# Tail of the single head's scores as two bfloat16 matmuls over three-part splits

## The chip, the cores and the metric

The kernel runs on one core of one Trainium2 chip. The metric is device time in microseconds (us) of one execution. Five engines run their own instruction streams and meet at semaphores: PE (TensorE, matrix multiplies; PEld is its loading of weights), DVE (VectorE), ACT (ScalarE), POOL (GpSimd, here the engine that issues the row gathers) and SP (SyncE, here the engine that issues all other transfers; SPq is its queue). Transfers run on 16 DMA engines.

## The reference

A graph of 12,500 nodes and 200,000 edges, the edges sorted by destination. Three message-passing steps follow one another: an attention pooling, a transformer convolution with 8 heads, and one with a single head of width 128.

```python
h = relu(layernorm(x));  x = x + pooled(h)            # step 1: softmax over edges of logit[src]
h = relu(layernorm(x));  x = x + conv1(relu(conv8(h)))
# a convolution, per edge s -> d with edge features e (16 numbers):
q, k, v = h @ Wq + bq, h @ Wk + bk, h @ Wv + bv
alpha = sum(q[d] * (k[s] + e @ We)) / sqrt(C)          # the score
w = softmax over the edges of d (alpha)
out[d] = sum(w * (v[s] + e @ We)) + h[d] @ Ws + bs
```

For the single head the kernel folds the key weights into the query: the score of an edge is the product of a column of 145 numbers of node `d` (128 against `h[s]`, 16 against `e`, one against a constant 1) and the row of the edge. The 128 are the main part, the 17 (`TAIL`) the tail.

## The kernel before

**Stages.** The program is written out in full, stage after stage, with a barrier between them: `prepare`, `hidden_stage`, `dense_stage("pool")`, `project_stage`, `edge_stage("multi")`, `fold_stage`, `dense_stage("single")`, `output_stage`.

**Dense stages.** Edges are cut into 391 blocks of 512 (`J` = 4 groups of 128), nodes into 98 tiles of 128. An item is a pair of a block and a tile that share edges; there are 488, in the order of the edges. Since low-numbered nodes have most of the edges, an item is nearly a block of its own at first, and a block has more and more items towards the end. POOL gathers the source rows, four gathers a block (L1155), into a ring of 8 blocks, as far ahead as the ring has room (it waits for `rows`, the copy by ACT at L1300 of the last item of the block that it overwrites). Everything else goes by item and is software-pipelined over up to three items: in `"single"` PE turns the rows (`ps_r`, L1265), makes the scores from `cols` (128x128) and `rowT` (L1251) plus `cols_tail` and `edge_tail` (L1253, 17 rows deep, float32), turns the weights (`ps_t`, L1278) and sums (`ps_p`, L1271); DVE does mask, minimum, copy and accumulation; ACT the exponentials and copies. In `"pool"` the scores are only a transpose (L1258).

**Transfers.** SP issues five transfers an item in `"single"`, in this order: `dst` (L1178), `cols` (L1183), `cols_tail` (L1185), `edge_tail` (L1189, 17 rows of 2 KB), the edge attributes (L1191). It runs at most four items (`QB`) ahead of the scores, since `cols` waits for the score of item n - 4; `dst` and the edge buffers are 8 deep (`U`).

**Fold.** `fold_stage` goes over 14 batches of 7 node tiles (`ROWS_B`). For a batch, SP loads `skip` and `x` (L1557, L1558), DVE makes `h` (L1585 to L1603), PE turns it (L1625), and multiplies; ACT copies `hT` (L1651), and then, for the batch before, `query_main` and `query_tail` (L1657, L1658). SP stores `h`, `x`, `query_main` and `query_tail` of the batch before (L1562 to L1568). SP loads a batch only when all four stores of two batches earlier have landed (L1556): a store and a load of one buffer share a semaphore's count.

Of the kernel before, what the change touches and what calls it, by code (L numbers as in the profile page):

```python
# [22 lines left out]
BF16 = mybir.dt.bfloat16  # L23
# [3 lines left out]
ds = bass.ds  # L27
# [32 lines left out]
DEN_EPS = 1e-16  # L60
assert ITEMS % U == 0 and NODE_TILES % ROWS_B == 0 and BATCHES % 2 == 0

# [89 lines left out]
def buffers(g):  # L152
# [14 lines left out]
    g.query_cols = scratch("query_cols", [SLOTS, ACC_W, P])  # L167
# [237 lines left out]
def hidden_stage(g):  # L405
# [8 lines left out]
    with ExitStack() as ph:  # L414
# [22 lines left out]
        def _(sp):  # L437
# [10 lines left out]
            sp.dma_start(g.query_cols[NODE_TILES, D:ACC_W, :], zero_cols[0:TAIL, :]).then_inc(s_w, 16)  # L448
# [5 lines left out]
            sp.wait_ge(s_w, 80)  # L454
# [211 lines left out]
def edge_stage(g, kind, rows, width, heads, ring_blocks):  # L666
# [404 lines left out]
    for k in EDGE_SIGNALS:  # L1071
        used = {"kv": multi, "attrT": multi, "edge": multi, "attrT_sb": multi, "scaled": multi,
                "prod": not pool_k, "alpha": not pool_k, "query": not pool_k, "onehot32": multi, "rows": not multi}.get(k, True)
        E[k].base += ITEMS if used else 0
# [15 lines left out]
def dense_stage(g, kind, rows, width, ring_blocks):  # L1090
# [16 lines left out]
    with ExitStack() as ph:  # L1107
# [10 lines left out]
        if single:  # L1118
            rowT = sb(g, ph, "rowT", [P, 2, EDGES_B])
            cols = sb(g, ph, "cols", [P, QB, P])  # L1120
            cols_tail = sb(g, ph, "cols_tail", [TAIL, QB, P])
            edge_tail = sb(g, ph, "edge_tail", [TAIL, U, EDGES_B])
            ps_r = [pb(g, ph, f"ps_r{k}", [P, EDGES_B]) for k in range(2)]
        ps_s = [pb(g, ph, f"ps_s_{kind}{k}", [P, EDGES_B]) for k in range(2)]
# [45 lines left out]

        @block.sync
        def _(sp):
            items = Items(g, sp, 0)

            def step(n, u):
                b = items.block(u)
                E["mask"].wait(sp, n - U)
                sp.dma_start(dst[:, u], t["dst_rows"][ds(b, 1), :].to_broadcast([P, EDGES_B]))\  # L1178
                  .then_inc(g.block_words_loaded[u], 16)
                if single:  # L1180
# [4 lines left out]
                    sp.dma_start(cols_tail[:, u % QB],  # L1185
                                 g.query_cols[ds(tile, 1), D:ACC_W, :].rearrange("t c n -> (t c) n"))\
# [7 lines left out]
            rolled(sp, ITEMS, U, 0, step, items.begin)  # L1194

        @block.vector
        def _(dve):
            items = Items(g, dve, 2)
            if single:
                V.memset(row[:, :, :, ACC_W - 1:ACC_W], 1.0)  # L1200
            V.memset(g.acc[:], 0.0)
# [3 lines left out]
            def step(n, u):  # L1205
# [26 lines left out]
                if has(m1, ITEMS):  # L1232
# [3 lines left out]
                     .then_inc(E["probT_sb"].sem, 1)  # L1236
            rolled(dve, ITEMS, U, 2, step, items.begin)

        @block.tensor
        def _(pe):  # L1240

            def step(n, u):
# [3 lines left out]
                if has(m1, ITEMS):  # L1246
                    E["low"].wait(pe, m1 - 2)
                    if single:
                        E["rowT_sb"].wait(pe, m1)
                        landed(pe, g.query_loaded, query_base, m1, u1, 32)  # L1250
# [544 lines left out]
```

## Time and profile before

| | |
|---|---|
| three runs | 10781.99, 10849.4 and 10866.37 us, median 10849.4 |
| span of the profiled execution (first to last instruction) | 7414.1 us |
| PE busy in the span | 5718.3 us (77%) |
| DVE, ACT, POOL busy | 4663.7 (63%), 3438.6 (46%), 4576.5 us (62%) |
| moved by DMA | 861.45 MB, mean 116 GB/s |

The span holds the instructions of the program. The difference to the run time, 3435.3 us, lies around it, and no view of the profile shows anything of it. The profiled execution's own device time is not listed apart. Busy shares are averages over stages that differ, so the stages have to be read one by one. Times below are counted from the span's start.

### The profile page before, as it was taken

Reading aid. Unit: us, or ns where it says so; the run is one execution under the profiler, and the core shown is the slowest. Engines: PE = TensorE matmul, PEld = TensorE weight load, DVE = VectorE, ACT = ScalarE, POOL = GpSimd, SP = SyncE. Lnnn points to the kernel's source line nnn. Section 1 sums busy time; section 2 is a strip of 40 time slices with the busy share of each in tenths; the row PEclk is TensorE's granted clock in tenths of the full one; section 3 lists DMA queues with packets and bytes.
Section 4 is the critical chain, followed back from the end, with each engine's and each line's share of the span. In section 5 each row is a group of like instructions: output and inputs, shape, how many; then the busy total and the mean of one; then the engine's idle time right before and its main releaser. Section 6 shows DMA issues by size and latency. Waiting matters only on the chain. (4 is left out here: it accounts for less than half of the span.)

```text
span 7414.1 us, 172328 instructions
## 1 busy us (share of the span) xinstructions
PE 5718.3 (77%) x38285; PEld 4085.0 (55%) x38285; DVE 4663.7 (63%) x12926; ACT 3438.6 (46%) x8180; POOL 4576.5 (62%) x4707
## 2 busy tenths in 40 slices
PE   4555566666665688888888888856889999999998
PEld 3455555555542466666666666633555556666666
DVE  4444555555665788999999999933444555555542
ACT  3233333333443466666666666612444444444441
POOL 0777777777750477777666665502777777777630
PEclk7777878888986799999999999977999999999995
DMA  2334444444434666666655555534445555555532
GB/s 81 85 82 83 85 85 87 88 89 89 92 90 140 161 155 157 159 158 153 151 144 145 142 140 137 130 103 119 108 110 112 117 116 119 123 122 123 119 88 60
DMA packets 1267854, 861.45 MB, mean 116 GB/s; under 512 B 637234, under 2 KB 1158320, under 8 KB 1266840
## 3 DMA queue, kind: packets, MB, share of 16 engines
q1 hardware_dynamic: 1091672, 438.53, 25.3%
q0 software_dynamic: 175168, 411.90, 23.7%
q8 instruction: 332, 5.44, 0.3%
q14 instruction: 682, 5.59, 0.3%
HBM read 780.46 MB, written 69.42 MB: 115 GB/s over the span
## 5 line engine op out<-in xcount | busy, mean ns | idle before, releaser
L757 POOL DMA_INDIRECT ring_multi<-kv_rows,src_cols x1564 | 1609.3, 1029 | 1029.7 <-issue 440.4
L1155 POOL DMA_INDIRECT ring_single<-h_rows,src_cols x1564 | 1482.6, 948 | 857.2 <-issue 480.3
L1155 POOL DMA_INDIRECT ring_pool<-pool_rows,src_cols x1564 | 1482.0, 948 | 678.6 <-issue 451.5
L1258 PE MATMUL ps_s_pool<-ident,row_pool 128*128 128x128 f32 x1952 | 365.1, 319 | 718.0 <-ACT row_pool L1300 716.8
L1300 ACT ACTIVATE row_pool<-ring_pool 128x520 f32 x488 | 309.1, 633 | 1162.1 <-POOLq L1146 1162.1
L958 PE MATMUL ps_e_multi<-w_edge,attrT 64*128 64x512 f32 x976 | 544.5, 638 | 331.4 <-DVE kv L847 310.9
L1222 DVE CUSTOM_DVE_ANT_0 masked_pool<-mask_pool,ps_s_pool,start_pool 128x512 f32<-128x512 bf16 x488 | 364.8, 748 | 633.4 <-PE ps_s_pool L1258 552.3
L1271 PE MATMUL ps_p_pool<-row_pool,probT_pool 128*128 128x129 f32 x3904 | 667.1, 325 | 55.2 <-DVE probT_pool L1235 54.2
L847 DVE TENSOR_TENSOR kv<-ring_multi,ps_e_multi 128x1024 f32<-128x1024 f32 x488 | 596.1, 1222 | 161.6 <-issue 124.0
L1258 PEld LDWEIGHTS ps_s_pool<-ident,row_pool 128*128 128x128 f32 x1952 | 254.1, 160 | 801.5 <-issue 764.9
L1305 ACT ACTIVATE rowT<-ps_r 128x512 f32<-128x512 f32 x488 | 291.7, 598 | 816.4 <-PE ps_r L1265 816.4
L1271 PEld LDWEIGHTS ps_p_pool<-row_pool,probT_pool 128*128 128x128 f32 x3904 | 602.7, 235 | 97.5 <-DVE probT_pool L1235 97.2
L1222 DVE CUSTOM_DVE_ANT_0 masked_single<-mask_single,ps_s_single,start_single 128x512 f32<-128x512 bf16 x488 | 364.7, 747 | 427.8 <-PE ps_s_single L1253 424.3
L948 PE MATMUL ps_p_multi<-message_multi,onehot 128*128 128x136 f32 x3904 | 584.2, 297 | 0.5 <-issue 0.4
L1271 PE MATMUL ps_p_single<-row_single,probT_single 128*128 128x145 f32 x3904 | 581.1, 292 | 2.4 <-DVE probT_single L1235 2.4
L1253 PE MATMUL ps_s_single<-edge_tail,cols_tail 17*128 17x512 f32 x976 | 549.7, 643 | 0.0
L948 PEld LDWEIGHTS ps_p_multi<-message_multi,onehot 128*128 128x128 f32 x3904 | 536.7, 207 | 0.9 <-issue 0.7
L1271 PEld LDWEIGHTS ps_p_single<-row_single,probT_single 128*128 128x128 f32 x3904 | 525.2, 194 | 3.6 <-DVE probT_single L1235 2.8
L1251 PE MATMUL ps_s_single<-rowT,cols 128*128 128x512 f32 x976 | 512.2, 607 | 1.5 <-issue 1.5
L1230 DVE SCALAR_TENSOR_TENSOR acc<-acc,factor_single,ps_p_single 128x145 f32 x488 | 178.9, 367 | 521.0 <-PE ps_p_single L1271 513.4
L1265 PEld LDWEIGHTS ps_r<-ident,row_single 128*128 128x128 f32 x1952 | 207.9, 142 | 493.1 <-issue 255.7
L1300 ACT ACTIVATE row_single<-ring_single 128x512 f32 x488 | 304.2, 623 | 294.5 <-POOLq L1146 292.0
(218 smaller groups left out, 12218.1 us busy)
## 6 DMA issues: line engine op xcount, KB each, us to landing
dst_pool<-in_dst_rows SPq DMA_DIRECT2D x488, 128.0 KB
dst_multi<-in_dst_rows SPq DMA_DIRECT2D x488, 128.0 KB
dst_single<-in_dst_rows SPq DMA_DIRECT2D x488, 128.0 KB
query_multi<-query_parts SPq DMA_DIRECT2D x488, 96.0 KB
cols<-query_cols SPq DMA_DIRECT2D x488, 64.0 KB
ring_pool<-pool_rows,src_cols POOLq DMA_INDIRECT x1564
ring_multi<-kv_rows,src_cols POOLq DMA_INDIRECT x1564
ring_single<-h_rows,src_cols POOLq DMA_INDIRECT x1564
```

Source lines behind the costliest of these rows:

```text
L757: pool.indirect_dma_start(out=ring[:, u, j, :], out_offset=None, in_=rows, in_offset=bass.IndirectOffsetOnAxis(ap=g.src_cols[:, c:c + 1], ...
L847: V.tensor_tensor(out=kv[:, u1 % 4], in0=in_ring(items.block(m1), 0, 2 * D).rearrange("p j (a c) -> p j a c", a=2), in1=ps_e[:].rearrange( ...
L948: i = T_.matmul(ps_p[:, 0:acc_w], lhs, rhs, start=(j == 0), stop=(j == J - 1))
L958: T_.matmul(ps_e[:], attrT[:, u % 2], w_edge[:].rearrange("k j c -> k (j c)"), start=True, stop=True).then_inc(E["edge"].sem, 1)
L1155: pool.indirect_dma_start(out=ring[:, u, j, :], out_offset=None, in_=rows, in_offset=bass.IndirectOffsetOnAxis(ap=g.src_cols[:, c:c + 1], ...
L1222: V.tensor_tensor_reduce(out=masked[:, p], in0=mask[:, p], in1=ps_s[p][:], scale=1.0, scalar=start[:, p], op0=ALU.add, op1=ALU.min, accum_ ...
L1251: T_.matmul(ps_s[p1][:], cols[:, u1 % QB], rowT[:, p1], start=True, stop=False)
L1253: T_.matmul(ps_s[p1][:], cols_tail[:, u1 % QB], edge_tail[:, u1], start=False, stop=True)\
L1258: i = T_.transpose(ps_s[p1][:, j * P:(j + 1) * P], row[:, u1, j, D + 1:D + 2].to_broadcast([P, P]), g.ident[:])
L1271: i = T_.matmul(ps_p[p3][:, 0:acc_w], probT[:, p3, j], row[:, u3, j, 0:acc_w], start=(j == 0), stop=(j == J - 1))
L1300: S_.activation(row[:, u, :, 0:copied], in_ring(items, u, 0, copied), ACT.Copy)\
L1305: S_.activation(rowT[:, u % 2], ps_r[u % 2][:], ACT.Copy).then_inc(E["rowT_sb"].sem, 1)
```

## The change

The tail's factors are each written as a sum of three bfloat16 numbers (`SPLIT` = 3: the number rounded, the rest rounded, the rest of that). All nine products are summed by two matmuls in bfloat16: `tail_a` (99 rows: the first and the second part of the query, each against the edge's three parts, and three rows against ones) and `tail_b` (48 rows: the third part of the query against the edge's three parts).

- **Single:** the float32 matmul of L1253 is replaced by two bfloat16 ones. SP issues six transfers an item in place of five: `cols`, `tail_a` (99 rows of 256 bytes), `tail_b` (48 rows of 256 bytes), and `edge_tail` as 96 rows of 1 KB, which reads the same 48 rows of `edge_parts` twice by a source pattern whose outer dimension is 2 with step 0. PE waits for DVE's clearing of buffers before its first item.
- **Pool:** between the items, every 12th, one of 40 chunks (128 x 626 numbers) of the edge attributes is loaded (SP, 12.8 MB in all), split in two ACT copies and two DVE subtractions, and stored (SP, 19.2 MB in all).
- **Fold:** after `query_tail`, DVE makes its three parts in five operations on 17 x 896 numbers, and SP stores them in 12 transfers a batch in place of one; loads wait for three stores in place of four.
- **Inputs:** `edge_cols` (17 x 200,192 float32, 13.61 MB) gives way to `edge_flat` (128 x 25,040 float32, 12.82 MB).

```diff
@@ dense_stage, single
-            cols_tail = sb(g, ph, "cols_tail", [TAIL, QB, P])
-            edge_tail = sb(g, ph, "edge_tail", [TAIL, U, EDGES_B])
+            tail_a = sb(g, ph, "tail_a", [TAIL_A, QB, P], BF16)
+            tail_b = sb(g, ph, "tail_b", [SPLIT_K, QB, P], BF16)
+            edge_tail = sb(g, ph, "edge_tail", [TAIL_A, U, EDGES_B], BF16)
...
+                i = chunk(n, 0)
+                if i is not None:
+                    if i >= 2:
+                        sp.wait_ge(third_done, i - 1)
+                    sp.dma_start(whole[:, i % 2], t["edge_flat"][:, i * CHUNK_W:(i + 1) * CHUNK_W])\
+                      .then_inc(split_loaded[i % 2], 16)
+                i = chunk(n, 18)
+                if i is not None:
+                    sp.wait_ge(third_done, i + 1)
+                    sp.dma_start(split_rows[:, :, i * CHUNK_W:(i + 1) * CHUNK_W], split[:, i % 2])\
+                      .then_inc(split_stored[i % 2], 16)
...
-                    sp.dma_start(edge_tail[:, u], t["edge_cols"][:, ds(b * EDGES_B, EDGES_B)])\
-                      .then_inc(g.attrs_loaded[u], 16)
+                    sp.dma_start(edge_tail[0:2 * SPLIT_K, u], g.edge_parts[:, ds(b * EDGES_B, EDGES_B)]
+                                 .unsqueeze(0).to_broadcast([2, SPLIT_K, EDGES_B])).then_inc(g.attrs_loaded[u], 16)
...
-                        T_.matmul(ps_s[p1][:], cols_tail[:, u1 % QB], edge_tail[:, u1], start=False, stop=True)\
+                        T_.matmul(ps_s[p1][:], tail_a[:, u1 % QB], edge_tail[:, u1], start=False, stop=False)
+                        T_.matmul(ps_s[p1][:], tail_b[:, u1 % QB], edge_tail[0:SPLIT_K, u1], start=False, stop=True)\
                           .then_inc(E["score"].sem, 1)
@@ fold_stage, SP
                     sp.dma_start(tiles[0:D], main[:, v]).then_inc(stored[v], 16)
-                    sp.dma_start(tiles[D:ACC_W], tail[:, v]).then_inc(stored[v], 16)
+                    sp.wait_ge(tail_part, 5 * (k + 1))
+                    rows = g.query_tails[k * ROWS_B:(k + 1) * ROWS_B].rearrange("t c n -> c t n")
+                    for a in range(SPLIT):
+                        for r in range(SPLIT):
+                            at = (a * SPLIT + r) * EDGE_DIM + (SPLIT if a == SPLIT - 1 else 0)
+                            sp.dma_start(rows[at:at + EDGE_DIM], tails[0:EDGE_DIM, v, a]).then_inc(tails_stored[v], 16)
+                        at = 2 * SPLIT_K + a
+                        sp.dma_start(rows[at:at + 1], tails[EDGE_DIM:TAIL, v, a]).then_inc(tails_stored[v], 16)
@@ fold_stage, DVE
+                    D_["query_done"].wait(dve, k)
+                    V.tensor_copy(tails[:, v, 0], tail[:, v]).then_inc(tail_part, 1)
+                    for a in range(SPLIT - 1):
+                        V.tensor_tensor(out=tail[:, v], in0=tail[:, v], in1=tails[:, v, a], op=ALU.subtract)\
+                         .then_inc(tail_part, 1)
+                        V.tensor_copy(tails[:, v, a + 1], tail[:, v]).then_inc(tail_part, 1)
```

PE, where the single stage has come into step (an item's rows, its scores, the sums of three items earlier, the weights of two earlier). Before:

```order
L1265 MATMUL ps_r<-ident,row_single 128x128 x4
L1278 MATMUL ps_t_single<-ident,prob_single 128x128 x4
L1251 MATMUL ps_s_single<-rowT,cols 128x512
L1253 MATMUL ps_s_single<-edge_tail,cols_tail 128x512
L1265 MATMUL ps_r<-ident,row_single 128x128 x4
```

After:

```order
L1323 MATMUL ps_r<-ident,row_single 128x128 x4
L1336 MATMUL ps_t_single<-ident,prob_single 128x128 x4
L1308 MATMUL ps_s_single<-rowT,cols 128x512
L1310 MATMUL ps_s_single<-edge_tail,tail_a 128x512
L1311 MATMUL ps_s_single<-edge_tail,tail_b 128x512
L1323 MATMUL ps_r<-ident,row_single 128x128 x4
```

Nothing moved; one row of the tail became two. SP, one batch of `fold_stage` (names are tensors in memory and buffers; `query_tails_sb` are the three parts), before:

```order
L1557 DMA skip<-skip_rows 128x7x128
L1558 DMA x<-x_rows 128x7x128
L1562 DMA h_rows<-h 128x7x128
L1564 DMA skip_rows<-x 128x7x128
L1567 DMA query_cols<-query_main 128x7x128
L1568 DMA query_cols<-query_tail 17x7x128
```

After:

```order
L1628 DMA skip<-skip_rows 128x7x128
L1629 DMA x<-x_rows 128x7x128
L1633 DMA h_rows<-h 128x7x128
L1635 DMA skip_rows<-x 128x7x128
L1638 DMA query_cols<-query_main 128x7x128
L1644 DMA query_tails<-query_tails_sb 16x7x128 x3
L1646 DMA query_tails<-query_tails_sb 7x1x128
L1644 DMA query_tails<-query_tails_sb 16x7x128 x3
L1646 DMA query_tails<-query_tails_sb 7x1x128
L1644 DMA query_tails<-query_tails_sb 16x7x128 x3
L1646 DMA query_tails<-query_tails_sb 7x1x128
L1628 DMA skip<-skip_rows 128x7x128
```

Twelve rows now stand between the store of `query_main` and the next batch's loads, where one stood. DVE in the same batch, the end of a batch, after the change:

```order
L1682 TENSOR_TENSOR x<-x,bs 128x896
L1689 TENSOR_TENSOR x<-x,ps_z 128x896
L1694 CAST query_tails_sb<-query_tail 17x896
L1697 TENSOR_TENSOR query_tail<-query_tail,query_tails_sb 17x896
L1700 CAST query_tails_sb<-query_tail 17x896
L1697 TENSOR_TENSOR query_tail<-query_tail,query_tails_sb 17x896
L1700 CAST query_tails_sb<-query_tail 17x896
L1664 TENSOR_SCALAR den<-acc 128x56
```

Before, `den` followed the addition of `ps_z` to `x` (L1689, which was L1610) directly; the five rows between are new.

## Rows read from the trace of the kernel before

**Rows 1.** Busy time by stage: stretch, length, each engine's busy (instructions), clock, DMA, GB/s
```profile
178.00:2178.00 2000.00, 1221.86 (x7837) 1095.43 (x7836) 1082.62 (x2959) 711.58 (x1467) 1482.03 (x1564) 0.84 0.41 86
...
5120.00:7200.00 2080.00, 1968.11 (x9760) 1209.04 (x9760) 1077.23 (x2931) 959.65 (x1952) 1482.64 (x1564) 0.98 0.53 115
```

**Rows 2.** The same view, stretches inside the single stage
```profile
5130.00:5700.00 570.00, 496.51 (x2343) 304.07 (x2343) 261.39 (x707) 238.95 (x474) 422.65 (x447) 0.94 0.50 110
5700.00:6300.00 600.00, 573.82 (x2844) 352.45 (x2842) 311.32 (x855) 281.25 (x568) 443.43 (x468) 0.98 0.54 117
6300.00:6900.00 600.00, 600.00 (x3058) 368.97 (x3058) 333.31 (x916) 295.53 (x612) 445.75 (x471) 1.00 0.56 123
6900.00:7142.00 242.00, 242.00 (x1230) 148.16 (x1229) 133.89 (x370) 117.93 (x245) 163.21 (x173) 1.00 0.54 118
```

**Rows 3.** Waits of POOL, single stage, then pool stage: total, times, longest
```profile
POOL ring_single L1155 <- issue: 480.3, 1468, 3.0
POOL ring_single L1155 <- ACT row_single L1300: 34.7, 30, 2.3
...
POOL ring_pool L1155 <- issue: 450.0, 1435, 2.0
```

**Rows 4.** Timeline: ends of the pool stage and of the single stage, start and length
```profile
2162.89 0.95 POOL L1155 DMA_INDIRECT ring_pool<-pool_rows,src_cols  x1 [0.30 <-issue]
2177.01 0.35 DVE L1230 SCALAR_TENSOR_TENSOR acc<-acc,factor_pool,ps_p_pool 128x129 f32 x1 [1.53 <-PE ps_p_pool L1271]
...
7141.74 0.95 POOL L1155 DMA_INDIRECT ring_single<-h_rows,src_cols  x1 [0.30 <-issue]
7198.21 1.26 PE L1271 MATMUL ps_p_single<-row_single,probT_single 128*128 128x145 f32 x8 [1.59 <-DVE probT_single L1235]
```

**Rows 5.** Timeline of PE: one item, and bfloat16 matmuls of the multi stage
```profile
6502.69 1.02 PE L1251 MATMUL ps_s_single<-rowT,cols 128*128 128x512 f32 x2
6503.64 1.12 PE L1253 MATMUL ps_s_single<-edge_tail,cols_tail 17*128 17x512 f32 x2
6504.70 0.66 PE L1265 MATMUL ps_r<-ident,row_single 128*128 128x128 f32 x4
6506.62 1.02 PE L1251 MATMUL ps_s_single<-rowT,cols 128*128 128x512 f32 x2
...
4755.39 0.83 PE L994 MATMUL ps_q_multi<-query_multi,onehotT_multi 128*128 128x128 bf16 x12
```

**Rows 6.** SP from 6300 to 6900: its wait, and from its timeline two issues
```profile
SPq L1183 <- PE ps_s_single L1253: 139.6, 149, 1.2
...
6501.70 0.25 SPq L1185 DMA_DIRECT2D cols_tail<-query_cols  x1
6502.15 0.25 SPq L1189 DMA_DIRECT2D edge_tail<-in_edge_cols  x1
```

**Rows 7.** DMA queues from 6300 to 6900: packets, MB, share of 16 engines
```profile
q1 hardware_dynamic: 129826, 41.72, 32.3%
```

**Rows 8.** Timeline of a batch of the fold stage: stores, then the next loads
```profile
4986.56 0.38 SPq L1567 DMA_DIRECT2D query_cols<-query_main  x1
4986.99 0.41 SPq L1568 DMA_DIRECT2D query_cols<-query_tail  x1
4992.63 0.37 SPq L1557 DMA_DIRECT2D skip<-skip_rows  x1
4993.65 0.56 SPq L1562 DMA_DIRECT2D h_rows<-h  x1
4997.96 0.25 DVE L1585 TENSOR_SCALAR den<-acc 128x56 f32<-128x56 f32 x1 [13.79 <-DMA x<-x_rows]
```

**Rows 9.** Fold stage: SP's wait for stores, and two groups of DVE by line
```profile
SPq L1556 <- DMA query_cols<-query_tail: 61.5, 12, 5.2
...
L1592 DVE TENSOR_TENSOR h<-acc,den 128x896 f32<-128x896 f32 x14 | 15.3, 1093 | 1.8
L1601 DVE TENSOR_SCALAR h<-h 128x896 f32<-128x896 f32 x14 | 8.8, 627 | 0.5
```

More of the change, by code:

```diff
@@ L60 @@
 DEN_EPS = 1e-16
+SPLIT = 3
+SPLIT_K = SPLIT * EDGE_DIM
+CHANNEL = EDGES + P
+FLAT = EDGE_DIM * CHANNEL // P
+CHUNK_W = 626
+SPLITS = FLAT // CHUNK_W
+EVERY = 12
+TAIL_A = 2 * SPLIT_K + SPLIT
+TAIL_ROWS = TAIL_A + SPLIT_K
 assert ITEMS % U == 0 and NODE_TILES % ROWS_B == 0 and BATCHES % 2 == 0
+assert SPLITS * CHUNK_W == FLAT and (SPLITS - 1) * EVERY + 18 < ITEMS
 def rolled(eng, total, unroll, lag, step, begin=None, peel=None):
@@ L1169, in landed, with chunk @@
             eng.wait_ge(sems[u % len(sems)], n * per + (per_item - (u % len(sems)) * per + base))
+        def chunk(n, at):
+            i, r = divmod(n - at, EVERY)
+            return i if not single and r == 0 and 0 <= i < SPLITS else None
         @block.sync
@@ L1194, in _ @@
             rolled(sp, ITEMS, U, 0, step, items.begin)
+            if not single:
+                for k in range(2):
+                    sp.wait_ge(split_stored[k], 16 * len(range(k, SPLITS, 2)))
         @block.vector
@@ L1236, in step @@
                      .then_inc(E["probT_sb"].sem, 1)
+                i = chunk(n, 5)
+                if i is not None:
+                    dve.wait_ge(first_done, i + 1)
+                    V.tensor_tensor(out=whole[:, i % 2], in0=whole[:, i % 2], in1=split[:, i % 2, 0], op=ALU.subtract)\
+                     .then_inc(first_off, 1)
+                i = chunk(n, 9)
+                if i is not None:
+                    dve.wait_ge(second_done, i + 1)
+                    V.tensor_tensor(out=split[:, i % 2, 2], in0=whole[:, i % 2], in1=split[:, i % 2, 1],
+                                    op=ALU.subtract).then_inc(third_done, 1)
             rolled(dve, ITEMS, U, 2, step, items.begin)
@@ L1240, in _ @@
         def _(pe):
+            if single:
+                pe.wait_ge(g.acc_clear, 3)
             def step(n, u):
@@ L1305, in step @@
                         S_.activation(rowT[:, u % 2], ps_r[u % 2][:], ACT.Copy).then_inc(E["rowT_sb"].sem, 1)
+                i = chunk(n, 3)
+                if i is not None:
+                    act.wait_ge(split_loaded[i % 2], 16 * (i // 2 + 1))
+                    if i >= 2:
+                        act.wait_ge(split_stored[i % 2], 16 * (i // 2))
+                    S_.activation(split[:, i % 2, 0], whole[:, i % 2], ACT.Copy).then_inc(first_done, 1)
+                i = chunk(n, 7)
+                if i is not None:
+                    act.wait_ge(first_off, i + 1)
+                    S_.activation(split[:, i % 2, 1], whole[:, i % 2], ACT.Copy).then_inc(second_done, 1)
             rolled(act, ITEMS, U, 2, step, items.begin)
@@ L1312, in dense_stage @@
     g.attrs_base += ITEMS * 32 // U if single else 0
-    g.query_base += ITEMS * 32 // QB if single else 0
+    g.query_base += ITEMS * 48 // QB if single else 0
 def waits_of_buffer(eng, sems, base, n, u):
@@ L1526, in fold_stage @@
         tail = sb(g, ph, "query_tail", [TAIL, 2, ROWS_B, P])
+        tails = sb(g, ph, "query_tails_sb", [TAIL, 2, SPLIT, ROWS_B, P], BF16)
+        tail_part = sem(g, "tail_part")
+        tails_stored = [sem(g, f"tails_stored{k}") for k in range(2)]
         wq = sb(g, ph, "wq2", [P, D])
```

49 lines of the change are left out of this document (35 added, 14 removed).

## Prediction

> **What bounds the kernel now.** I read the busy time by stage first [rows 1]. The single stage takes 2080 us of the 7414.1 us span, PE is busy in 1968 of them, and the change takes work from PE: that looks like a large gain. The pool stage corrects the picture: POOL issues the same 1564 gathers there, is busy for the same 1482 us, and that stage lasts 2000 us with PE busy in only 1222. A gather costs POOL 0.95 us and some 0.3 us up to the next [rows 4], so about 1.27 us, or 5.1 us a block. That alone is 1990 us of the single stage.
>
> Then the single stage in stretches [rows 2]. An item has 20 matmul records on PE (4 for `ps_r`, 2 and 2 for the scores, 4 for `ps_t`, 8 for `ps_p`), so the four stretches hold 117, 142, 153 and 61.5 items: 4.87, 4.22, 3.92 and 3.93 us an item. The gathers go at 78.4, 78.0, 78.5 and only in the last stretch at 71.5 per 100 us. So gathers set the pace up to 6300 us; from there PE is busy all the time and falls behind, the ring of 8 blocks takes up the lag, and only near the end does POOL wait for a freed block: 34.7 us in 30 waits [rows 3]. The rest of the lag is the drain: from the end of the last gather (7142.7 us) to the last item 57 us in the single stage, in the pool stage 13 us (2163.8 to 2177) [rows 4].
>
> So the most that a faster item can bring: some 8 gathers lie ahead of 5130 us (the stage starts at 5120) and 447 + 468 up to 6300; 641 are left. At 600/471 = 1.274 us each [rows 2] they end at 7117, with the pool stage's drain 7130, against 7199.5 now: **70 us**. In items: 488 - 117 - 142 = 229 are left after 6300 us and take 900 us now, 3.93 each. With p us an item the stage ends 900 - 229 p earlier, up to 70 us (p = 3.62 or less). Before 6300, p up to 4.2 costs nothing.
>
> **The change, part by part.** *Scores.* The tail's float32 matmul holds PE from 6503.64 to 6504.70, 1.05 us [rows 5]; it is four passes of 512 columns in two records. Two bfloat16 matmuls are two passes. Twelve bfloat16 ones of 128 columns take 0.83 us, 69 ns each with their weights [rows 5]; by columns that is at most 0.28 us for 512, so 0.55 for two; the least is half of the tail's time less its overheads, 0.45. I take 0.5, which saves 0.55: PE alone would need 3.4 us an item. The Trainium skill, "TensorE: Matmul & The Clock Gate", section "Back-to-back issue gap", gives N / 2.4 + 2.5 ns warm; by it the two take 0.43 us and PE would need 3.3 us. No row here has a bfloat16 matmul of 512 columns.
>
> *SP in the single stage.* From 6300 to 6900 us SP waits 139.6 us over 153 items, 0.91 us each [rows 6], so it works 3.0 us an item. One transfer more costs the spacing of `cols_tail` and `edge_tail`, 0.45 us [rows 6], and the two larger ones some 0.05 each: 3.55 us. SP passes from 23% to almost no slack, and becomes the next limit at the end, just where it is enough (3.62).
>
> *The copy of the edges.* 34 KB an item become 96 KB. I leave a margin for it and for waits that come when nothing has slack: p = 3.75, a gain of 900 - 859 = **41 us**. Bounds: 70, and nothing at p = 3.93.
>
> *More traffic.* The chunks add 32 MB to the pool stage, the tails and edges 91 KB an item (44 MB) to the single stage, 16 and 21 GB/s on 86 and 115 [rows 1]. The gaps that go to issue are 450.0 us in the pool stage at a DMA share of 0.41 and 480.3 in the single stage at 0.53 [rows 1, 3]. 30 us for 0.12; the new traffic is about 0.05 in each: up to 12 us. I take **+6** twice; bounds 0 and 12. The chunks' two ACT copies and two DVE subtractions each 12 items lie beside POOL's gathers, which leave PE, ACT and DVE 39% and more idle there [rows 1]; without that cover they would cost some 40 x 3 us.
>
> *Fold.* Here nothing hides anything. Per batch SP stores `query_main` at 4986.56 and `query_tail` at 4986.99, waits for the landing, and loads the next but one at 4992.63: 6.07 us [rows 8]; the wait is 61.5 us in 12 batches [rows 9]. DVE then idles until 4997.96 for that load. The wait goes, since loads ask for three stores only and that of `query_main` lands meanwhile. In its place, in order on SP: 0.42 for `query_main`; DVE's five operations, which start when `query_tail` is there, 3 casts and 2 subtractions of 896 numbers, a subtraction 1.09, a cast between 0.63 and 1.09 [rows 9], so 4.1 to 5.5, and 0.3 for the hand-overs; then 12 issues, nine at 0.41 (as `query_tail`'s) and three at 0.25 [rows 6, 8], each 0.05 apart: 5.0. Together 9.8 to 11.2 against 6.07. I take +4.2 for 12 batches, 50 us, and 9 for the last, whose tail now follows the DVE work: **+59 us**. Bounds: 12 issues at 0.25 and cheap casts, +2.2 a batch and 33 us in all; 12 at 0.56 [rows 8] and dear casts, +7.4 and 101 us. Queued behind SP's new wait are the next loads, for which all engines wait. DVE, waiting for `query_tail`, has nothing else due before that load.
>
> **Sum.** -41 + 59 + 6 + 6 = +30 us on the span of 7414.1. The profiled execution's 3435.3 us outside the span are taken as unchanged, and the median of the runs stands for its time: 10849.4 + 30, about **10,880 us**.
>
> **Rivals.**
> (a) *Slower: the copy of `edge_tail` becomes the bound.* If its rows don't spread over the 16 DMA engines, one engine carries much of 96 rows. For it: the source pattern has an outer dimension of 2. With two engines, 48 rows of 1 KB each. A packet of q1 takes 32.3% x 16 x 600 us / 129,826 = 23.9 ns at a mean of 321 bytes [rows 7]; 1 KB costs between that and 76 ns (by bytes), so 1.15 to 3.7 us. An engine has now 0.56 x 3.92 = 2.2 us an item [rows 2]. Sum 3.3 to 5.9 us; at 4.4 the stage ends 229 x 4.4 - 900 = 108 later, and 142 x (4.4 - 4.22) = 25 more: +133 in place of -41, in all +204, **11,053 us**; at 5.9 about 800. It makes the kernel over 1% slower from p = 4.1 on. Against it: transfers 8 deep hide any latency, and the lower half of the price is below what PE takes now. The Trainium skill, "DMA: Bandwidth & Descriptors", section "Why a DMA increments its semaphore by 16 and not by 1", says that the engine count is the largest number up to 16 that divides the slowest dimension of both patterns, which would be 2 here (and 1 for the present copies of 17 rows). No row shows the count.
> (b) *The gain is whole and fold cheap.* Spread copy, p under 3.62, fold at its lower bound: -70 + 33 = **10,812 us**. Against it: SP at 3.55.
> (c) *The time around the span shrinks.* The inputs lose 0.79 MB of some 42 MB in and out. If the 3435 us went by bytes, that is 65 us: **10,815 us**. Nothing in the profile speaks for or against it.
> (d) *PE's clock.* It is 0.98 to 1.00 in the last stretches and 0.94 where PE is busy for 87% of the time [rows 2]. If the shorter item lets it fall to 0.94 at the end, 3.4 becomes 3.6 us: within the forecast.
>
> **How the numbers follow.** Forecast 0.62 (all within 1%), (a) 0.2, (b) 0.1, (c) 0.08. Over 1% (108 us) is about what can be told from no change. Slower by that: (a), and a fold at its upper bound together with no gain, 0.21. Faster: (b) and (c) together, 0.04. Within: 0.75. The range reaches down a little beyond (b) and (c) and up to the middle of (a): 10,790 to 11,030; the forecast's own is 10,810 to 10,950.
>
> **What would show it.** In the single stage: two records of 0.25 us for the tail; an item at 3.6 to 3.9 us after 6300; gathers at 78 per 100 us to the end, POOL's waits for ACT's rows under 10 us; a drain of 20 to 40 us. SP's wait for the scores gone there. If instead PE waits for a DMA of `edge_tail`, (a) holds. In the fold stage: each batch 3 to 5 us longer, SP's wait names DVE and not the stores. In the pool stage: the same length within 15 us. The prediction is wrong if PE was the real pace before 6300 (the stage would then shrink by far more than 70 us), or if a chunk's store holds up gathers.

## The result, and the profile after

| | median of 20 runs | range |
|---|---|---|
| kernel before | 10850.4 us | 10777.6 to 10905.6 |
| changed kernel | 10877.4 us | 10817.3 to 10934.5 |

The ratio is 1.0036, 95% interval 1.0019 to 1.0053: taken on 10,850 us, 39 us more, between 21 and 58 (the two medians by themselves differ by 27). The change is below 1% and the time is inside the range of the prediction; its +30 is inside the interval.

The profile after shows at once that much of the prediction's ground does not hold for these runs. The changed kernel's profiled execution takes 10889.8 us and its span is 10888.0 us. So next to nothing (1.8 us) lies around the span; the 3435.3 us that the section on the time before put around the span, and that the prediction left "outside", are inside, in the stages with gathers. The execution that the rows of before were read from was an untypical one: a second profile of the unchanged kernel (`b0` below) has a span of 10601.3 us in 10603.2.

Busy time by stage, pool, multi and single (the columns as in [rows 1]). The changed kernel:

```profile
190.00:3107.00 2917.00, 1349.82 (x7800) 1213.56 (x7800) 1123.05 (x3009) 753.28 (x1544) 1490.03 (x1564) 0.71 0.30 69
3405.00:7105.00 3700.00, 2625.23 (x19030) 1952.44 (x19031) 2233.82 (x5861) 1542.46 (x4393) 1529.97 (x1564) 0.72 0.37 94
7448.00:10674.00 3226.00, 2157.79 (x9758) 1381.34 (x9759) 1070.82 (x2930) 955.50 (x1952) 1480.52 (x1564) 0.81 0.39 88
```

The same view of `b0`, the unchanged kernel:

```profile
192.00:3055.00 2863.00, 1355.77 (x7807) 1219.45 (x7808) 1070.03 (x2929) 699.82 (x1464) 1477.53 (x1564) 0.71 0.27 60
3352.00:6936.00 3584.00, 2600.01 (x19031) 1938.11 (x19032) 2232.29 (x5858) 1538.93 (x4393) 1521.99 (x1564) 0.73 0.39 97
7215.00:10388.00 3173.00, 2481.77 (x9759) 1480.57 (x9760) 1073.73 (x2929) 948.08 (x1952) 1478.05 (x1564) 0.81 0.33 75
```

In `b0` the busy times of DVE, ACT and POOL are within 2% of those of [rows 1]; PE's is 11% larger in the pool stage and 26% in the single stage, at a lower clock. The pool stage is 2863 us long in place of 2000, the single stage 3173 in place of 2080. POOL is busy for 52% and 47% of them, not for 74% and 71%. (The two profiles are from different chips. On the one of the result the kernel before takes 10,850 us, on the one of `b0` 10,573, so stages are compared only within a chip.)

Waits in the single stage, the changed kernel, then `b0` (total, times, longest):

```profile
ACT rowT L1363 <- remote: 1415.8, 171, 20.3
POOL ring_single L1178 <- ACT row_single L1358: 1225.4, 214, 12.4
...
PE ps_s_single L1310 <- DMA row_single<-in_edge_attr: 37.5, 32, 2.9
...
SPq L1230 <- PE ps_p_single L1329: 14.1, 31, 0.7
SPq L1230 <- remote: 0.5, 3, 0.2
SPq L1217 <- DVE mask_single L1257: 0.3, 1, 0.3
```

```profile
POOL ring_single L1155 <- ACT row_single L1300: 1132.2, 190, 11.1
ACT rowT L1305 <- remote: 1105.2, 140, 30.3
...
SPq L1183 <- PE ps_s_single L1253: 514.3, 272, 4.1
SPq L1183 <- remote: 336.2, 114, 5.0
```

Three things are to be seen. POOL waits over 1100 us for a free block (34.7 in [rows 3]), so in these runs its gathers don't set the pace. ACT waits over 1100 us for `ps_r` with nothing in the profile that is still at work, which the view calls remote. And SP, which waits 852 us in the single stage of `b0`, waits 15 us in all after the change.

What "remote" is, in the timeline of the changed kernel (start, length, [idle before]):

```profile
9000.08 0.60 PE L1336 MATMUL ps_t_single<-ident,prob_single 128*128 128x128 f32 x4
9001.38 0.38 PE L1310 MATMUL ps_s_single<-edge_tail,tail_a 99*128 99x512 bf16 x1
9001.69 0.39 PE L1311 MATMUL ps_s_single<-edge_tail,tail_b 48*128 48x512 bf16 x1
9002.01 0.66 PE L1323 MATMUL ps_r<-ident,row_single 128*128 128x128 f32 x4
9007.18 0.69 DVE L1280 COPY probT_single<-ps_t_single 128x512 f32<-128x512 f32 x1 [5.58 <-remote]
9009.44 0.60 ACT L1363 ACTIVATE rowT<-ps_r 128x512 f32<-128x512 f32 x1 [8.25 <-remote]
```

The transposes into `ps_t` are recorded as done at 9000.68, those into `ps_r` at 9002.67. The semaphores with which PE tells so rise at 9007.15 and 9009.42, and DVE and ACT start 0.03 us later. From 9002.67 to 9007.15 no compute engine works. Counting each rise of a semaphore that comes over 1 us after the end of the record it belongs to:

| | pool | multi | single |
|---|---|---|---|
| PE, execution of [rows 1 to 9] | 0 | 0 | 0 |
| PE, `b0` | 548 | 1245 | 689 |
| PE, changed kernel | 528 | 1146 | 747 |
| DVE, all three | 0 | 0 | 0 |

The end of a matmul's record is modelled, so the trace can't tell whether PE's signal is late or the matmul itself stands still. The Trainium skill, "Perfetto Trace Analysis", section "Tensor Engine Instruction (MATMUL, LD_WEIGHTS)", says the same of the recorded end: an estimate from size and delay, not an observation. Below, "late" means late against the record. The traces also lack some of the rises (12% to 21% of PE's in the ordinary executions, 3% in that of [rows 1 to 9], about 30% of DVE's in `b0` and the changed kernel), so the counts are lower bounds.

### The profile page after: what moved, and what is told of

The parts are those of the page before. It is cut to its first block and busy times, and to the rows that moved or that the text cites. A ratio compares the mean times of both kernels' runs of the same rounds, so it can differ in the third digit from the quotient of the medians.

```text
span 10888.0 us, 173824 instructions
## 1 busy us (share of the span) xinstructions
PE 6690.3 (61%) x38285; PEld 4886.5 (45%) x38285; DVE 4855.3 (45%) x13077; ACT 3475.6 (32%) x8260; POOL 4503.1 (41%) x4707
## 5 line engine op out<-in xcount | busy, mean ns | idle before, releaser
L971 PE MATMUL ps_e_multi<-w_edge,attrT 64*128 64x512 f32 x976 | 754.1, 863 | 859.4 <-ACT attrT L1051 551.2
L1349 ACT ACTIVATE prob_pool<-masked_pool,low_pool 128x512 f32<-128x512 f32 x488 | 352.2, 722 | 2016.3 <-DVE low_pool L1267 1722.2
L1329 PE MATMUL ps_p_single<-row_single,probT_single 128*128 128x145 f32 x3904 | 710.8, 334 | 388.4 <-DVE probT_single L1280 310.5
L961 PE MATMUL ps_p_multi<-message_multi,onehot 128*128 128x136 f32 x3904 | 760.0, 357 | 0.5 <-issue 0.4
L961 PEld LDWEIGHTS ps_p_multi<-message_multi,onehot 128*128 128x128 f32 x3904 | 719.7, 267 | 0.8 <-issue 0.6
L971 PEld LDWEIGHTS ps_e_multi<-w_edge,attrT 64*128 64x128 f32 x976 | 187.0, 238 | 1004.7 <-ACT attrT L1051 799.1
L1275 DVE SCALAR_TENSOR_TENSOR acc<-acc,factor_pool,ps_p_pool 128x129 f32 x488 | 170.1, 348 | 1038.2 <-remote 795.9
L1007 PE MATMUL ps_q_multi<-query_multi,onehotT_multi 128*128 128x128 bf16 x5856 | 572.2, 270 | 0.0
L1280 DVE COPY probT_single<-ps_t_single 128x512 f32<-128x512 f32 x488 | 336.1, 689 | 500.5 <-remote 431.0
L1063 ACT ACTIVATE absent_multi<-ps_m_multi,neg_big 128x4 f32<-128x4 f32 x488 | 128.7, 264 | 1203.4 <-PE ps_m_multi L998 705.3
```

The source lines that it names most:

```text
L961: i = T_.matmul(ps_p[:, 0:acc_w], lhs, rhs, start=(j == 0), stop=(j == J - 1))
L971: T_.matmul(ps_e[:], attrT[:, u % 2], w_edge[:].rearrange("k j c -> k (j c)"), start=True, stop=True).then_inc(E["edge"].sem, 1)
L1007: i = T_.matmul(ps_q[:, j], onehotT[:, u, j], query[:, u % QB, k, 0:D], start=(k == 0), stop=(k == 2))
L1275: V.scalar_tensor_tensor(out=a2, in0=a2, scalar=factor[:, f2], in1=ps_p[p2][:, 0:acc_w], op0=ALU.mult, op1=ALU.add).then_inc(E["summed"].s ...
L1280: V.tensor_copy(probT[:, p1].rearrange("p j n -> p (j n)"), ps_t[p1][:])\
L1329: i = T_.matmul(ps_p[p3][:, 0:acc_w], probT[:, p3, j], row[:, u3, j, 0:acc_w], start=(j == 0), stop=(j == J - 1))
```

## The experiments

Stage lengths below run from the first gather (or the end of the stage ahead) to the last `ps_p` matmul or the next first gather. The first four kernels ran on one chip (before: 10,572.6 us), the next four on one where before took 10,567.8 us, the last four on one with 10,818.6 us. A stage's length is from the one profiled execution of a kernel, the ratio from all its runs. The unchanged kernel was profiled on the first chip only; on the second, `notail` has before's pool and multi stages, and they take 2861 and 3576 us there against `b0`'s 2863 and 3585, so `b0`'s stages are used for the second chip too.

**What each part of the change costs.** `b0` is the kernel before:

> The kernel before, unchanged. Two theories on the time that the profile of before did not show. (O) outside: the 3435 us lie around the instructions; then this execution's span is again near 7414 us while its time is near 10,850 us. (W) waits: the profiled execution of before was an untypical one, and ordinary ones have the 3435 us inside, as stalls in which PE, DVE, ACT and SP all do nothing for 2 to 9 us, as the changed kernel's profile shows them (span 10,888.0 us of a time of 10,889.8 us); then span and time differ by some 2 us, the pool stage takes near 2,900 us and not 1,985, and the single stage near 3,200 us.

Theory W holds: the span is 10,601.3 us of 10,603.2, the pool stage takes 2863 us and the single stage 3174.

`nofold` leaves the twelve stores and the five DVE operations out and fills the tails with zeros ahead; `nochunk` the chunks; `neither` both.

```diff
@@ nofold, fold_stage
-                    V.tensor_copy(tails[:, v, 0], tail[:, v]).then_inc(tail_part, 1)
...
-                            sp.dma_start(rows[at:at + EDGE_DIM], tails[0:EDGE_DIM, v, a]).then_inc(tails_stored[v], 16)
@@ nochunk, dense_stage
-            return i if not single and r == 0 and 0 <= i < SPLITS else None
+            return None
```

> The changed kernel without the chunks of the pool stage (the edge parts are an input of zeros) and without the three parts of the query's tail (they stay zero, written once in the hidden stage): the scores' tail is left out of the computation, the single stage does all its transfers and matmuls. It shows the change in the single stage by itself. Prediction's theory (gathers set the pace, PE's gain 41 us, traffic +6): 35 us faster than before, ratio 0.997. Rival 1 (stalls set the pace and shrink with the work on PE's path): 0.5 us less an item on 488 items, 240 us faster, ratio 0.978. Rival 2 (one more transfer an item on SP, whose register instructions take 0.7 us in places, costs what PE gains): ratio 1.000 to 1.01.

> The changed kernel without the three parts of the query's tail in the fold stage (no five DVE operations and no 12 stores a batch; the tails stay zero). Prediction's theory: the fold stage returns to its time of before and this is 59 us faster than the changed kernel (ratio to before 0.998). Rival (the fold stage has the same time as its loads wait in either): equal to the changed kernel, ratio 1.0036.

> The changed kernel without the 40 chunks of the pool stage (the edge parts are an input of zeros). Prediction's theory: hidden behind the gathers, 6 us, ratio 1.003. Rival (the pool stage isn't bound by the gathers but by waits among PE, ACT and DVE, and each chunk puts some 3 us on them): 40 to 120 us faster than the changed kernel, ratio 0.993 to 1.000.

| us | ratio to before, 95% | hidden | pool | multi | fold | single |
|---|---|---|---|---|---|---|
| `b0` | 1 | 192 | 2863 | 3585 | 278.4 | 3174 |
| `neither` | 1.0029 (1.0010 to 1.0049) | 234 | 2876 | 3619 | 239.3 | 3200 |
| `nofold` | 1.0022 (1.0004 to 1.0040) | 232 | 2853 | 3562 | 243.7 | 3168 |
| `nochunk` | 1.0075 (1.0052 to 1.0097) | 194 | 2879 | 3595 | 342.5 | 3204 |

- The fold stage costs +64.1 us. Without splits and stores it is 35 to 39 us shorter than before, so these alone cost 99 to 103. The removed wait for `query_tail` by itself is worth about 20 of the 35 to 39: `paced_best` below, which drops only that wait, has 258. `nofold` and `neither` also lack the one store of the tail; the rest was not taken apart.
- The single stage, the same program in all three, is 5 us shorter to 30 us longer than before. The multi stage, which is before's own, differs by -23 to +34 between executions, so that is within noise. The runs say the same: the ratios less what the fold and hidden stages account for leave +28, +18 and +13 us for all the rest, each within some 20 to 25. A gain of 41 us from the two bfloat16 matmuls does not show on this chip.
- The chunks cost nothing that these runs show (pool 2853 with, 2876 and 2879 without; by the runs, `nofold` with them and `neither` without have ratios of 1.0022 and 1.0029). `nochunk` itself, at 1.0075, is outside what either theory expected, and above the changed kernel's 1.0036, which was measured on another chip. The +40 in the hidden stage is the filling with zeros, which only `nofold` and `neither` have.

**Is PE's work on the path?** `notail` is the kernel before without the float32 matmul of the tail.

```diff
-                        T_.matmul(ps_s[p1][:], cols[:, u1 % QB], rowT[:, p1], start=True, stop=False)
+                        T_.matmul(ps_s[p1][:], cols[:, u1 % QB], rowT[:, p1], start=True, stop=True)
-                        T_.matmul(ps_s[p1][:], cols_tail[:, u1 % QB], edge_tail[:, u1], start=False, stop=True)\
```

> The kernel before without the tail's float32 matmul (the 17 rows of the tail are left out of the scores; all transfers, waits and copies stand). It takes 1.05 us an item from PE, twice what the change takes, 488 x 1.05 = 512 us in all. Theory A (the single stage's items wait for late signals and not for PE's work): under 100 us shorter. Rival D (PE's work is on the path of every item): 400 to 510 us shorter, about 10,100 us, and the change should then have gained about 250.

The stage in `notail`, then in `nochunk`, the changed program's:

```profile
7205.00:10245.00 3040.00, 1837.08 (x8784) 1348.45 (x8784) 1069.30 (x2929) 958.38 (x1952) 1481.88 (x1564) 0.78 0.34 79
7303.00:10507.00 3204.00, 2161.49 (x9752) 1388.55 (x9752) 1073.42 (x2930) 954.77 (x1952) 1478.52 (x1564) 0.80 0.40 89
```

Ratio 0.9878 (0.9843 to 0.9913), single stage 3041 us in place of 3174. PE's busy time falls by 645 us and the stage by 133, a fifth. That is between what both theories expected: neither "nothing" nor "all" holds. For the change, which takes 320 us of busy time off PE (2161.5 in `nochunk` against 2481.8), a fifth would be 66 us. Whether something takes them back or they are lost among the late signals, these kernels don't tell.

**What makes the late signals?** They occur only in stages with gathers, and in `b0`'s pool stage the share of time with no compute engine at work is at most 0.01 where POOL was busy with gathers for less than 30% of the last 5 us, 0.39 where it was for 60 to 70% and 0.61 for 70 to 80%. So three kernels put a pause between gathers: `pace_short` and `pace_long` on the kernel before (384 and 896 numbers), `pace_after` on the changed one (384).

```diff
                     ).then_inc(gathered[n % 2][j], 16)
+                    if g.pauses >= 2:
+                        pool.wait_ge(g.paused, g.pauses - 1)
+                    pool.memset(pause[:, g.pauses % 2], 0.0).then_inc(g.paused, 1)
+                    g.pauses += 1
```

> The kernel before with a pause on POOL: after every gather of the pool, multi and single stages POOL clears a scratch row of 384 numbers (one partition; by the row of the clearing of 488 numbers, 0.50 us, and of 128, 0.19 us, about 0.4 us). Gathers then start at least some 1.6 us apart in place of 1.25. Nothing else is changed. Theory A (gathers that follow each other without a pause hold up what the other engines tell each other): the idle stretches of 2 to 9 us in which no compute engine works become few; pool stage 2550 to 2700 us (it was 2863), single stage 2600 to 2900 (3174), multi 3000 to 3400 (3585), in all 9,400 to 10,300 us. Rival B (each gather costs the others the same wherever it stands): the same number of gathers, the same idle time: 10,500 to 10,700 us. Rival C (POOL is the pace and its waits for a free block are no slack): 1564 x 0.35 us more in each of three stages, 12,000 us and over.

> As the short pause, with a cleared row of 896 numbers, about 0.9 us: gathers at least 2.1 us apart. Theory A: the idle stretches are gone nearly wholly, but POOL alone now needs 1564 x 2.1 = 3300 us a stage, so about 10,900 us in all, with PE's longest waits in the dense stages for POOL's blocks. Rival B: the idle stretches stay and add to that, 11,500 us and over.

> The changed kernel with the short pause. Theory A: it gains what the kernel before gains from the same pause, and what the change does is seen with few stalls: fold stage again 60 to 65 us longer than before; the single stage, where PE is a larger part of the time, 0 to 100 us shorter than that of the kernel before with the pause. Rival B: as the changed kernel, 10,600 to 10,700 us on this chip.

POOL's timeline, `b0`, then `pace_short`:

```profile
1499.16 0.94 POOL L1155 DMA_INDIRECT ring_pool<-pool_rows,src_cols  x1 [0.30 <-issue]
1500.41 0.94 POOL L1155 DMA_INDIRECT ring_pool<-pool_rows,src_cols  x1 [0.30 <-issue]
```

```profile
1500.35 0.95 POOL L1163 DMA_INDIRECT ring_pool<-pool_rows,src_cols  x1 [0.16 <-issue]
1501.29 0.41 POOL L1169 MEMSET pause_pool<- 1x384 f32 x1
1501.86 0.95 POOL L1163 DMA_INDIRECT ring_pool<-pool_rows,src_cols  x1 [0.16 <-issue]
```

| | us | ratio to before, 95% | period of gathers | pool | multi | single | late in pool, multi, single |
|---|---|---|---|---|---|---|---|
| `b0` (first chip) | 10603, one run | 1 | 1.25 | 2863 | 3585 | 3174 | 548, 1245, 689 |
| `pace_short` | 9386 | 0.8853 (0.8813 to 0.8894) | 1.52 | 2412 | 3469 | 2526 | 6, 1083, 730 |
| `pace_long` | 10336 | 0.9766 (0.9724 to 0.9808) | 1.95 | 3061 | 3227 | 3072 | 0, 0, 0 |
| `pace_after` | 9732 | 0.9187 (0.9154 to 0.9220) | 1.52 | 2424 | 3514 | 2757 | 9, 1006, 1133 |

Work was added to POOL, and the kernel became 11.5% faster (the interval is against before's runs on the same chip). Rivals B and C fall: with the same number of gathers, the time between them decides how late the signals are, and with 1.95 us none is late in any stage. Dense gathers are thus needed for late signals in these runs, but not enough by themselves: the execution of [rows 1 to 9] has them 1.25 us apart and no late signal. All pauses here are a cleared row on POOL; another way to space the gathers was not tried. With the long pause POOL is the pace (1564 x 1.95 = 3050 us). At 1.52 it depends on the stage: 6 in the pool stage, where 1564 x 1.52 = 2377 us set the time, many in multi and single. There the number hardly falls, but they are shorter: in the single stage 730 of them add up to 1469 us of lateness, where `b0`'s 689 add up to 2805. Not all of the expectation was met: pool and single came below their ranges, multi above, and `pace_long` took 10,336 us and not 10,900, its period being 1.95 and not 2.1 us.

The surprise is `pace_after`. Under the same pause the fold stage is 64 us longer, as expected, but in the single stage the change costs 231 us where 0 to 100 us of gain were expected. The busy time of the stage, `pace_short`, then `pace_after`:

```profile
6647.00:9173.00 2526.00, 2180.51 (x9760) 1322.42 (x9760) 1101.67 (x2930) 970.16 (x1952) 2125.26 (x3128) 0.91 0.42 95
```

```profile
6770.00:9527.00 2757.00, 2052.58 (x9760) 1309.32 (x9760) 1095.68 (x2930) 955.22 (x1952) 2131.76 (x3128) 0.88 0.48 103
```

PE has less to do and the stage is longer. In the first 60 items (from one accumulation by DVE to the 60th after it), with gathers equally dense in both (65.5 and 65.6 per 100 us), 20 signals are late before and 194 after, and an item takes 5.85 and 6.28 us. So the single stage of the changed kernel brings on late signals at a pace of gathers that the old one bears.

**Which part of it?** Three more kernels, all `pace_after` with one thing taken away or spread.

```diff
@@ pace_five
-                    sp.dma_start(tail_b[:, u % QB],
@@ pace_once
+                    sp.dma_start(edge_tail[0:SPLIT_K, u], g.edge_parts[:, ds(b * EDGES_B, EDGES_B)])\
@@ pace_spread
+                    for a in range(2):
+                        sp.dma_start(edge_tail[a * SPLIT_K:(a + 1) * SPLIT_K, u],
```

> The changed kernel with the short pause, without the transfer of tail_b (its 48 rows are cleared once and stay zero, so the third part of the query is left out of the scores; the matmul over them stands). SP issues five transfers an item in the single stage, as before the change. Measured so far with the short pause: single stage 2526 us before and 2757 us after the change. Theory E (each transfer that SP issues adds to the load that makes PE's signals late): 2560 to 2660 us. Theory F (the copy of the edges, 96 rows of 1 KB, does it): 2700 us and over. Theory G (PE's two bfloat16 matmuls or their order do it): unchanged, 2740 to 2770.

> The changed kernel with the short pause; the copy of the edges takes its 48 rows once and not twice (rows 48 to 95 stay at one, so the second part of the query is multiplied with ones and the scores are not the reference's). Six transfers an item stand; the copy is 48 KB in place of 96, and its source has no outer dimension of 2. Theory E: unchanged, 2720 to 2770 us in the single stage. Theory F: 2530 to 2650. Theory G: unchanged.

> The changed kernel with the short pause; the copy of the edges is two transfers of 48 rows each, the same bytes, seven transfers an item. Theory E: 2800 to 2900 us in the single stage. Theory F, if it is that the copy lies on few DMA engines: 2530 to 2700; if it is its bytes: 2757. The prediction's rival (a) is the first of these.

On this chip the late signals are a little more frequent: the multi stage, the same program, takes 3600 to 3625 us in place of 3514. Scaled by the two times of before (10,818.6 / 10,567.8), `pace_after`'s single stage would be about 2820 us here.

| | ratio to before, 95% | transfers, packets an item | single | late |
|---|---|---|---|---|
| `pace_short` (other chip) | 0.8853 | 5, 852 | 2526 | 730 |
| `pace_after` (other chip) | 0.9187 | 6, 1088 | 2757 (about 2820) | 1133 |
| `pace_five` | 0.9166 (0.9135 to 0.9197) | 5, 1025 | 2870 | 1130 |
| `pace_once` | 0.9110 (0.9075 to 0.9145) | 6, 1054 | 2803 | 1159 |
| `pace_spread` | 0.9159 (0.9127 to 0.9191) | 7, 1118 | 2824 | 1109 |

None of them recovers it. The number of transfers (theory E), the bytes of the edges' copy and the DMA engines that it lies on (theory F, and the prediction's rival (a)) are each out as the single cause. A part is not: `pace_once` is 17 us under the scaled 2820, and its ratio is below `pace_after`'s, without overlap of the two intervals, though on another chip. What is left are the two matmuls themselves (theory G, for which no kernel was made), the 99 rows of `tail_a` that replace 17, the number of SP's packets as a whole, which is 20% to 31% above before in all four, or several together; that was not separated, and stays open.

**Is SP the pace without the pause?** SP hardly waits any more. The part of an item's time in which it doesn't wait is (3173 - 852) / 488 = 4.76 us in `b0`, (3226 - 15) / 488 = 6.58 us after the change (6.36 in `nochunk`, on `b0`'s chip). But that is not the length of its list: in `notail`, whose transfers are those of `b0`, it is 5.7. Taking only items in which no SP instruction is slow and no gap falls between them, an item takes SP 2.92 us in the median in `b0` and 3.86 after the change (25 and 109 such items). So the longer list costs +0.94, and the rest is slow instructions.

SP's lead says how far this reaches PE. Between the issue of an item's last transfer and that item's scores on PE lie 19.3 us in the median in `b0` and 6.2 in the changed kernel's execution (4.3 in the third quarter of the items, and there under 0.1 at the least). In `nochunk` it is 15.5 in the median and never under 2.9, PE's matmuls wait for no transfer, and the single stage is as long as in `neither` (a lead of 10.7 us, and 35.4 us of waits for transfers). So SP has lost its slack, but it is not shown to set the pace, and where the gain of the matmuls goes stays open. SP's timeline in the changed kernel:

```profile
9504.25 0.01 SPq L1217 DMA_DIRECT2D dst_single<-in_dst_rows  x1
9509.24 0.01 SPq L1222 DMA_DIRECT2D cols<-query_cols  x1
9509.31 0.33 SPq L1224 DMA_DIRECT2D tail_a<-query_tails  x1
9509.83 0.33 SPq L1226 DMA_DIRECT2D tail_b<-query_tails  x1
9510.25 0.67 SPq L1230 DMA_DIRECT2D edge_tail<-edge_parts  x1
9511.13 0.41 SPq L1232 DMA_DIRECT2D row_single<-in_edge_attr  x1
9511.79 0.35 SPq L1217 DMA_DIRECT2D dst_single<-in_dst_rows  x1
9512.49 0.34 SPq L1222 DMA_DIRECT2D cols<-query_cols  x1
```

From 9509.31 to 9513.02, `tail_a` to `tail_a`, an item takes 3.7 us, and none of it is slow; just before, from the issue of `dst` at 9504.25 to that of `cols`, 5.0 us pass on slow instructions. In all, 1502 of SP's instructions in this stage take 0.5 to 0.9 us, register instructions that take 0.04 elsewhere among them (808 in `b0`, 11 in the execution of [rows 1], 2 in `pace_long`). They come with the late signals and go with them.

**A faster kernel.** `paced_best` is the kernel before with a pause of its own in each stage, and with loads in the fold stage that don't wait for `query_tail`.

```diff
+PAUSES = {"pool": 256, "multi": 704, "single": 448}
@@ fold_stage, SP
-                        sp.wait_ge(stored[u], (n - 2) * 32 + (64 - 32 * u))
+                        sp.wait_ge(stored[u], (n // 2) * 48)
```

> The kernel before with a pause of its own in each stage (rows of 256, 704 and 448 numbers in pool, multi and single; by the two pauses measured, a gather's period is 1.19 us + 0.84 ns a number: 1.41, 1.78 and 1.57 us), and in the fold stage loads that wait for three stores and not for that of query_tail. If PE's signals stay in time at these paces, the gathers set the stages: pool 2240, multi 2800 to 3000, single 2480 to 2540, fold 243 us; with 192, 296 and 214 for the rest some 8,500 to 8,750 us. If the pace of 1.41 is already too dense for the pool stage, 2400 to 2700 there.

```profile
189.00:2873.00 2684.00, 1407.93 (x7805) 1263.02 (x7806) 1080.00 (x2929) 699.80 (x1464) 1962.27 (x3128) 0.71 0.29 64
3169.00:6140.00 2971.00, 2345.96 (x19032) 1764.79 (x19032) 2162.19 (x5859) 1541.41 (x4393) 2688.81 (x3128) 0.80 0.47 117
6398.00:8887.00 2489.00, 2140.04 (x9760) 1338.27 (x9760) 1110.21 (x2929) 975.89 (x1952) 2212.94 (x3128) 0.91 0.43 96
```

9102 us against 10,819, ratio 0.8409 (0.8381 to 0.8436): 16% faster than before, where the changed kernel is level with before. It is above the 8,500 to 8,750 us expected. Multi and single came as expected (71 and 89 late signals). In the pool stage 1.41 us is too dense: 691 late, 2684 us, where the pause of 384 gives 2414 to 2420 on the same chip (in the changed kernel's variants). With that one the sum would be about 8,830 us, an estimate; it wasn't run. The fold stage takes 258 us in place of 278; 243 was expected.

## Why the prediction was right or wrong, point by point

**The total was right, for a sum of which one term was right; that it came so near is in part luck.** Measured +39 (21 to 58), predicted +30. The fold's +59 is +64. The single stage's -41 and +6 are together between -5 and +30, on another chip than the total's. The chunks' +6 in the pool stage is nothing within 25 us. The fold stage alone is more than the whole interval; what made the rest of the kernel some 25 us shorter (64 - 39) on the chip of the result was not found, since no ordinary execution of before was profiled there.

**Fold: right, with two errors that cancel.** From the store of `query_main` to the next load it is 10.84 us (9.8 to 11.2 predicted, 6.07 before [rows 8]). SP and DVE in a batch of the changed kernel:

```profile
7255.30 0.38 SPq L1638 DMA_DIRECT2D query_cols<-query_main  x1
7259.47 1.29 SPq L1644 DMA_DIRECT2D query_tails<-query_tails_sb  x3
7260.81 0.78 SPq L1646 DMA_DIRECT2D query_tails<-query_tails_sb  x1
...
7266.14 0.39 SPq L1628 DMA_DIRECT2D skip<-skip_rows  x1
```

```profile
7255.30 0.61 DVE L1694 CAST query_tails_sb<-query_tail 17x896 bf16<-17x896 f32 x1 [2.38 <-ACT query_tail L1749]
7255.95 1.08 DVE L1697 TENSOR_TENSOR query_tail<-query_tail,query_tails_sb 17x896 f32<-17x896 f32 x1
...
7258.83 0.62 DVE L1700 CAST query_tails_sb<-query_tail 17x896 bf16<-17x896 f32 x1
```

The casts are at the cheap end (0.61; five operations in 4.15 us, predicted 4.1 to 5.5). The twelve issues take 6.6 us and not 5.0, since those of `7x1x128` take 0.75 to 0.78 and not 0.25. The wait names DVE's last cast, as predicted, 50.3 us in 14 batches.

**"The 3435.3 us outside the span are taken as unchanged": the step that failed.** The sum survived it, the argument didn't. A span 31% shorter than every run should have cast doubt on the profiled execution; instead the missing time was placed around the span. With it three readings fell: gathers as the pace (POOL waits 1132 us for blocks), PE busy all the time from 6300 us on (it is busy for 78% of the stage), and PE's clock, 0.81 in the single stage of both kernels, where [rows 2] have 0.94 to 1.00.

**Scores: the saving is there on PE, and no gain in time shows.** The two matmuls follow each other, and the next, 0.31 and 0.32 us apart (9001.38, 9001.69, 9002.01 above): 0.63 us for the pair where 0.5 was taken and the float32 matmul takes 1.05. That is at a granted clock of 1.00, the 2.4 GHz level (347 of 488 items); at 0.50, the 1.2 GHz level (121 items), the pair takes 1.10 and the float32 one, in `b0`, 2.00. The Trainium skill ("TensorE: Matmul & The Clock Gate", section "Back-to-back issue gap") gives N / 2.4 + 2.5 ns for an isolated warm matmul, which makes 0.43 for the two, and adds that a stream of matmuls is faster than this formula at 512 columns; the trace has a longer spacing than the formula even so, with a weight load for each matmul, and the measurement decides. PE's busy time fell by 320 us, 0.66 an item at the clocks of these runs.

**SP: right that its slack goes, short in size.** It was named as the next limit, at 3.0 + 0.55 us an item. Undisturbed it went from 2.92 to 3.86, +0.94; with the slow instructions, from 4.76 to 6.4 or 6.6. The issue of `edge_tail` takes 0.67 us in the median and not 0.30, the larger part of what was missing. That it limits anything is not shown.

**Rival (a), the copy on few DMA engines, is out.** PE waits 37.7 us in all for transfers in this stage, and none in `nochunk`; and `pace_spread`, the same bytes in two copies of 48 rows, is not faster. How many engines the copy used can't be read from the trace. **Rival (b)** needed the whole gain; none showed. **Rival (c)** falls with the time around the span, which is 1.8 us. **Rival (d)**, a clock that sinks by the change: 0.81 and 0.80 after the change against 0.81 (changed kernel, `nochunk`, `b0`), so not by the change. Against [rows 2] it is lower in both kernels, and it differs with the pauses: 0.91 in `pace_short`'s single stage, 0.88 in `pace_after`'s.

## What to carry to other kernels

Compare the span of a profiled execution with the times of the runs before reading a bound from it; a span far below them describes an untypical execution, and the missing time has to be looked for inside an ordinary one. When waits name nothing that is at work, change the density of what runs beside them: here a pause that put 0.3 us more between the gathers of an engine that wasn't the bound was worth 11.5%, where leaving out a whole matmul an item on the engine that looked busiest was worth 1.2%. Work saved on a busy engine is worth only what an experiment like `notail` shows, here a fifth of it. Price also what the saving puts on other engines and stages: here +64 us in the fold stage, and SP's slack.

## What the runs showed of the hardware that was not expected

- With indirect gathers issued by POOL 1.25 us apart, PE's semaphores rise up to 26 us after the recorded end of its work (2805 us of lateness in all in `b0`'s single stage), none that is recorded of DVE's over 1 us, and SP's register instructions take 0.7 in place of 0.04 us. At 1.95 us between gathers, no signal is late and 2 of SP's instructions are slow. The pace that is borne depends on the stage: in the pool stage 1.52 us is nearly enough (6 late) and 1.41 is not (691), in multi 1.78 nearly is (71) and 1.52 is not (1083). Which path these share was not found.
- One execution of the unchanged program ran with gathers 1.25 us apart and no late signal at all, in 7414 us. The 57 timed runs of it on these chips took 10,531 us and more; what made this one so is open.
- Two bfloat16 matmuls of 512 columns, 99 and 48 rows deep, start 0.31 us apart at a granted clock of 1.00 (347 items of the changed kernel, 0.31 to 0.35) and 0.57 at 0.50 (121 items).
- DMA issues of the shape `7x1x128` hold SP for 0.75 us in the median (42 of them), those of `16x7x128` for 0.43 (126).
